# The first row of experts in another order: units 2 and 3 ahead of the two that are summed by tokens

## The chip, the cores and the metric

One Trainium2 chip, one of its NeuronCores. The metric is the device time of one execution in microseconds, as the median of several runs.

## What is computed

The reference is a small language-model tower over 8 rows (batches) of 512 tokens: an embedding with a decaying memory and four residual MLP layers of width 128; an output head to 64 features; linear attention with four heads; and a mixture of 8 experts, of which each token takes the best two. The change touches the experts alone:

```python
logits = jnp.einsum('bsd,de->bse', xn, Wr) + br
top_vals, top_idx = jax.lax.top_k(logits, K)
w = jax.nn.softmax(top_vals, axis=-1)
w_full = jnp.einsum('bsk,bske->bse', w, jax.nn.one_hot(top_idx, E, dtype=w.dtype))
y = jnp.zeros(x.shape[:-1] + (DOUT,), x.dtype)
for e in range(E):
    h = jax.nn.gelu(jnp.einsum('bsd,dh->bsh', xn, W1[e]) + b1[e], approximate=False)
    y_e = jnp.einsum('bsh,hd->bsd', h, W2[e]) + b2[e]
    y = y + y_e * w_full[..., e, None]
```

Every expert is computed for every token and weighted by its gate, which is zero for the six that were not chosen.

## The kernel before

The program is written out by hand, one instruction stream for each engine: TensorE (PE), VectorE (DVE), ScalarE (ACT), GpSimd (POOL) and SyncE, which issues the DMAs. The streams wait for each other by semaphores, and each engine works strictly in the order in which its stream is written. From the span's start to about 265 us the tower runs, then the attention of the eight rows, and from about 304 us the experts.

A **unit** is one expert of one row of 512 tokens: unit `n` is row `n // 8`, expert `n % 8`, 64 in all. An ordinary unit takes these steps:

- `hidden(n)` on PE: two 128x512 products with the high and the low part of the first weights, into bank 4 or 0 by turns. It waits until the gelu of unit n-2 has emptied its bank.
- `gelu(n)` on ACT (line 898), out of that bank.
- `spread_gates(n)` on PE: the expert's gates, spread over all 128 partitions by one 128x512 product with a selection column, into bank 2 or 3 by turns in the first two rows. It waits until the multiplication of the unit before it in that bank is done.
- `dve_job(n)` on DVE (line 1419): hidden times gates.
- `hidden_hi(n)` on ACT (line 904): the product rounded to fp32r.
- `hidden_lo(n)`: the remainder of the rounding, on DVE (line 1426) for even experts and on POOL (line 650) for odd ones.
- `second_products(n)` on PE: two 128x512 products, of the high and of the low part, added up over the experts of a row in bank 6 or 7. The row's `bias_sum` has to come first, since it opens that sum.

The streams go through laps, one for each unit. In lap `n` PE spreads the gates of unit n, issues `hidden(n + 6)` and the second products of unit n - 4 (SKEW is 4, LEAD is 6), and ACT does `gelu(n + 6)` and then the rounding of unit n - 1.

Four units are exceptions (`ALONE`): 0 and 1 at the start of the first row, and the last two of the last row. For these there is no spread, no multiplication, no rounding. PE multiplies the unrounded hidden values by the second weights with the tokens on the partitions (`alone_product`, here ahead of lap 0), into the two halves of bank 6, and DVE adds each with its gate per token straight to the output row (`alone_sum`, line 1445, four instructions). `alone_taken` says that DVE has done so. Since bank 6 is also the one in which row 0 adds up its experts, `bias_sum(0)` must wait for both sums.

In the kernel before, laps 0 and 1 have no spread and no multiplication, laps 4 and 5 have the two `alone_sum` on DVE and no second products on PE, and `bias_sum(0)` stands in lap 6. Around these laps the last work of attention is interleaved: `projected_context(7)`, `q_transposes(7)`, `attend(6)` and `attend(7)` on PE, `scaled_output(5)`, `residual_moments(5)` and `scaled_m(7)` on DVE (lines 1315, 1167 to 1170, 1301), the norm of row 5 on POOL, and the transposes of the gates of row 1 (`turn_gates(1)`, in lap 4).

Of the kernel before, what the change touches and what calls it, by code (L numbers as in the profile page):

```python
# [34 lines left out]
B, S, V = 8, 512, 64  # L35
# [9 lines left out]
SKEW = 4  # L45
# [32 lines left out]
UNITS = B * E  # L78
# [59 lines left out]
def alone(n):  # L138

    return n in ALONE  # L140


def alone_before(n):
# [49 lines left out]
def build(nc, tok_in, emb_in, wupd_in, wf_in, w1_in, w2_in, headw_in, cols_in, rows_in, cons_in,  # L193
          wqkv_in, wout_in, memv_in, wr_in, ew1_in, ew2_in, eb2_in, out_hbm):
    ctx = ExitStack()
    with ctx:
# [472 lines left out]
        def _(act):  # L669
# [277 lines left out]
            for n in range(UNITS + SKEW + 2):  # L947
                m, u = divmod(n, E)
                if u == SKEW + 1 and n >= E:
                    copy_sum(m - 1)  # L950
                if n + LEAD < UNITS:
                    gelu(n + LEAD)
                if 1 <= n <= UNITS and split(n - 1):
                    hidden_hi(n - 1)
                if n == 2:
                    q_turned(7, 1)
                if n == 5:
                    output_squares(6, 0)
                if n in (7, 8):
                    ez_of(5, 1, pair(n - 7))  # L960
                if n == E + 1:
                    ez_hi(5, 1)
                    output_squares(7, 1)
                if n == E + 5:
                    expert_z_turned(5)
                if n in (2 * E - 1, 2 * E):
                    ez_of(6, 0, pair(n - (2 * E - 1)))
                if n == 2 * E + 1:
                    ez_hi(6, 0)
                if n in (2 * E + 6, 2 * E + 7):  # L970
                    ez_of(7, 1, pair(n - (2 * E + 6)))
                if n == 2 * E + 7:
                    expert_z_turned(6)
                if n == 3 * E:
                    ez_hi(7, 1)
                if n == 4 * E - 3:
                    expert_z_turned(7)
                if n == 2 * E + 4:
                    gate(1)
                if n == 5 * E:  # L980
                    gate(2)
                if n in GATES_AT:
                    copy_gates(GATES_AT.index(n) + 1)
# [3 lines left out]
        def _(dve):  # L987
# [512 lines left out]

            for n in range(UNITS + E + 1):
                m, u = divmod(n, E)
                if n < UNITS and not alone(n):
                    dve_job(n)
                if n in (4, 5):
                    alone_sum(n - 4)
                if n == 1:
                    scaled_output(5, 1)
                if n == 2:
                    residual_moments(5, 1)  # L1510
                    scaled_m(7, 1, v_total[7])
                if n == 6:
                    output_sums(6, 0)
                if n == E:
                    scaled_output(6, 0)
                if n == E + 1:
                    residual_moments(6, 0)
                if n == E + 2:
                    expert_z_lo(5, 1)
                    output_sums(7, 1)  # L1520
                if n == E + 5:
                    scaled_output(7, 1)
                if n == E + 6:
                    residual_moments(7, 1)
                if n == 2 * E + 2:
                    expert_z_lo(6, 0)
                if n == 3 * E + 1:
                    expert_z_lo(7, 1)
                if n in (2 * E + 1, 4 * E + 3):
                    p = 1 if n < 3 * E else 2  # L1530
                    take_logits(p)
                    v = first_max(p)
                if n in (2 * E + 2, 4 * E + 5):
                    v = first_hot(p, v)
                if n in (2 * E + 3, 4 * E + 6):
                    v = second_max(p, v)
                if n in (2 * E + 4, 4 * E + 7):
                    v = second_hot(p, v)
                if n in (2 * E + 5, 5 * E + 1):
                    v = weights(p, v)  # L1540
                if n in (2 * E + 6, 5 * E + 2):
                    gates_out(p, v)
                if u == 0 and n == UNITS + E:
                    alone_sum(UNITS - 2)
                    alone_sum(UNITS - 1)
                if u == 0 and n >= 2 * E:
                    output(m - 2)
                if 1 <= n <= UNITS and lo_by_dve(n - 1):
                    hidden_lo(n - 1)


        @block.tensor
        def _(pe):
# [454 lines left out]
            for n in range(UNITS + SKEW + 4):  # L2008
                m, u = divmod(n, E)
                if n < UNITS:  # L2010
                    if u == 0:
                        pe.wait_ge(gates_copied, m + 1)
                    if n == E + SKEW:
                        pe.wait_ge(h1_ready, 7)
                    if not alone(n):
                        spread_gates(n)
                if n + LEAD < UNITS:
                    hidden(n + LEAD)
                if n == SKEW + 2:
                    pe.wait_ge(alone_taken, 2)  # L2020
                if n == SKEW + 2 or (u == SKEW and 0 < m < B):
                    bias_sum(m * E)
                if n == 0:
                    projected_context(7, 1)
# [5 lines left out]
                    attend(7, 1)  # L2030
                if n in GATES_AT:
                    turn_gates(GATES_AT.index(n) + 1)
                if SKEW <= n < UNITS + SKEW and not alone(n - SKEW):
                    second_products(n - SKEW)
                if n in (UNITS - 3, UNITS - 2):
                    alone_product(n + 1)
                if u == SKEW + 3 and n >= E:
# [75 lines left out]
```

## Time and profile before

| | us |
|---|---|
| median of 3 runs | 414.32 |
| lowest and highest of them | 412.72, 414.88 |
| the profiled execution's own time | 413.41 |
| its span in the trace | 411.6 |
| PE, DVE, ACT, POOL busy in it | 387.6, 351.5, 322.0, 257.1 |

The span runs from the first to the last instruction that the profile holds; 1.8 us lie around it. A row of a timeline gives the start in us from the span's start, how long the row's instructions took from the first start to the last end, the engine, the line, the operation with its output and inputs, their number, and in brackets the idle time ahead of it on that engine with what ended it. Instructions overlap a little, so the distance between two starts is shorter than the time of one. A row of a table of stretches gives the stretch, its length, then for PE, the loading of PE's weights, DVE, ACT and POOL the busy us with the number of instructions, then the mean granted clock of PE as a share of full speed, the share of DMA time and GB/s.

### The profile page before, as it was taken

What the parts mean: (1) busy time and instruction counts of PE and PEld (TensorE: products, weight loads), DVE (VectorE), ACT (ScalarE), POOL (GpSimd) and SP (SyncE); (2) the same over time, 40 slices, a digit from 0 to 9 for tenths busy, and PEclk for the clock granted to TensorE, in tenths of its full rate; (3) what the DMA queues carried; (4) which work ended last, traced back from release to release, by engine and by line L of the source; (5) the groups of instructions that cost most, each with busy time, mean ns of one, the idle gap of its engine ahead of it and who ended that gap; (6) DMA issues with size and microseconds to landing.
All of it is one profiled execution on the core that took longest, in us unless ns stands there. A gap on an engine that the chain in (4) does not pass through costs nothing.

```text
span 411.6 us, 6417 instructions
## 1 busy us (share of the span) xinstructions
PE 387.6 (94%) x2005; PEld 314.3 (76%) x2005; DVE 351.5 (85%) x863; ACT 322.0 (78%) x552; POOL 257.1 (62%) x386
## 2 busy tenths in 40 slices
PE   5698899999999999999999998999998899999995
PEld 2496578888888888888888887877887677786774
DVE  4887798888988898898888979999986899889886
ACT  1263599989999998898887765578787898997983
POOL 0575787778778879877787466586521554545451
PEclk9999999999999999999999999999999999999998
DMA  6900002212121211221222000000000000000001
GB/s 200 362 7 0 2 26 41 38 52 53 36 41 53 52 30 51 51 41 38 53 51 52 2 0 2 1 2 1 2 0 2 1 2 13 15 13 13 15 13 26
DMA packets 15850, 14.94 MB, mean 36 GB/s; under 512 B 9797, under 2 KB 10569, under 8 KB 15561
## 3 DMA queue, kind: packets, MB, share of 16 engines
q1 hardware_dynamic: 15816, 14.54, 14.0%
q8 instruction: 16, 0.26, 0.3%
q14 instruction: 18, 0.14, 0.1%
HBM read 13.42 MB, written 1.11 MB: 35 GB/s over the span
## 4 chain that ended last, share of the span: by engine, by line
PE 65%; DVE 18%; ACT 7%; issue 5%; DMA 3%; SPq 2%; POOL 0%; DVEq 0%; ACTq 0%
PE ps L1555 59%; PE ps L1578 4%; DMA hh<-in_tokens 3%; DVE hid L1419 2%; ACT w_all L904 2%; DVE x L1419 1%; ACT x L898 1%; DVE stats L1034 1%; DVE kstat L1255 1%; ACT hid L898 1%; SPq L451 1%; DVE x L1271 1%; DVE hh L1445 1%; DVE hh L1315 1%; DVE qmax L1267 1%
## 5 line engine op out<-in xcount | busy, mean ns | idle before, releaser
L1108 DVE TENSOR_TENSOR hid_lo<-hid,hid_hi 128x1024 fp32r<-128x1024 f32 x64 | 79.1, 1235 | 25.5 <-ACT hid_hi L742 25.4
L737 ACT ACTIVATE hid<-ps,b_fold 128x512 f32<-128x512 f32 x128 | 83.8, 681 | 20.3 <-PE ps L1555 19.9
L1555 PE MATMUL ps<-xn_hi,w_all 128*128 128x512 f32 x256 | 87.7, 403 | 0.7 <-DVE xn_lo L1103 0.6
L1555 PE MATMUL ps<-hid_hi,w_all 128*128 128x512 f32 x256 | 85.0, 393 | 0.0
L742 ACT ACTIVATE hid_hi<-hid 128x1024 fp32r<-128x1024 f32 x64 | 67.9, 1061 | 2.0
L1555 PEld LDWEIGHTS ps<-xn_hi,w_all 128*128 128x128 f32 x256 | 48.4, 189 | 11.2 <-issue 0.9
L1555 PEld LDWEIGHTS ps<-hid_hi,w_all 128*128 128x128 f32 x256 | 48.1, 188 | 9.9
L1555 PE MATMUL ps<-xn_lo,w_all 128*128 128x512 f32 x128 | 50.0, 390 | 0.0
L1555 PE MATMUL ps<-hid_lo,w_all 128*128 128x512 f32 x128 | 49.8, 389 | 0.0
L1555 PE MATMUL ps<-hid_hi,ew 128*128 128x512 f32 x128 | 40.6, 400 | 1.0 <-ACT memT L840 0.4
L1034 DVE BATCH_NORM_STATS2 stats<-ps 128x6 f32<-128x128 f32 x160 | 35.1, 280 | 3.3 <-PE ps L1578 3.3
L542 POOL TENSOR_TENSOR var_in<-var_in 128x4 f32<-128x4 f32 x30 | 34.2, 1141 | 2.4
L546 POOL TENSOR_TENSOR var_in<-var_in,mhalf 128x4 f32<-128x4 f32 x30 | 31.4, 1047 | 2.3
L538 POOL TENSOR_TENSOR var_in<-stats 128x4 f32<-128x4 f32 x30 | 17.2, 573 | 24.4 <-DVE stats L1034 24.4
L1578 PEld LDWEIGHTS ps<-cons,x 128*128 128x128 f32 x160 | 23.2, 187 | 9.8 <-DVE x L1053 4.4
L1578 PE MATMUL ps<-cons,x 128*128 128x128 f32 x160 | 25.4, 281 | 4.4 <-DVE x L1053 3.2
L1555 PE MATMUL ps<-w_all,ew 128*128 128x512 f32 x77 | 28.7, 413 | 0.8 <-DVE xn_lo L1426 0.2
L1555 PEld LDWEIGHTS ps<-hid_hi,ew 128*128 128x128 f32 x128 | 23.5, 188 | 6.8 <-ACT x L898 0.8
L1555 PEld LDWEIGHTS ps<-hid_lo,w_all 128*128 128x128 f32 x128 | 24.0, 188 | 4.8
L1555 PEld LDWEIGHTS ps<-xn_lo,w_all 128*128 128x128 f32 x128 | 24.1, 189 | 4.0
L904 ACT ACTIVATE w_all<-hid 128x512 fp32r<-128x512 f32 x39 | 24.8, 638 | 2.1 <-DVE hid L1419 2.0
L1555 PE MATMUL ps<-hid_lo,sel 128*128 128x512 f32 x60 | 25.4, 423 | 0.8 <-ACT hid_lo L884 0.4
(237 smaller groups left out, 914.5 us busy)
## 6 DMA issues: line engine op xcount, KB each, us to landing
rstd_row<-roots SPq DMA_DIRECT2D x29, 256.0 KB, 3.8
hh<-in_tokens SPq DMA_DIRECT2D x8, 256.0 KB, 8.3
hid<-in_w SPq DMA_DIRECT2D x1, 1024.0 KB, 7.7
rstd_row<-in_w SPq DMA_DIRECT2D x1, 1024.0 KB, 10.6
out<-hh SPq DMA_DIRECT2D x7, 128.0 KB, 2.0
ew_raw<-in_expert_w SPq DMA_DIRECT2D x1, 512.0 KB, 9.7
roots<-rstd SPq DMA_DIRECT2D x29, 2.0 KB, 1.4
ew_raw<-in_expert_w SPq DMA_DIRECT2D x1, 256.0 KB, 9.9
```

The costliest lines, as they stand in the source:

```text
L538: own.inc(pool.tensor_tensor(vi[:, 0, :], st[:, :, 1], st[:, :, 4], ALU.subtract))
L542: own.inc(pool.tensor_tensor(vi[:, 0, :], vi[:, 0, :], vi[:, 0, :], ALU.mult))
L546: v = own.inc(pool.tensor_tensor(vi[:, 0, :], vi[:, 2, :], mhalf[:, 0:NT], ALU.pow))
L737: act.activation(hid[:, j % 2, f, :], bank[f], ACT.Gelu, bias=b1_fold[:, j // B * F + f:j // B * F + f + 1]).then_inc(gelu_done, 1)
L742: act.activation(hid_hi[:, j % 2, 2 * p:2 * p + 2, :], hid[:, j % 2, 2 * p:2 * p + 2, :], ACT.Copy).then_inc(hhi_ready, 1)
L898: act.activation(hg(n % NHG), bank[HIDDEN_BANK[n % 2]], ACT.Gelu, bias=eb1_fold[:, n % E:n % E + 1]).then_inc(eg_done, 1)
L904: act.activation(hw_hi[:, slot * S:(slot + 1) * S], hw(slot), ACT.Copy).then_inc(hwhi_act, 1)
L1034: last = dve.bn_stats(stats6[:, slot, t, :], bank[TB][:, t * P:(t + 1) * P])
L1108: dve.tensor_tensor(hid_lo[:, j % 2, 2 * p:2 * p + 2, :], hid[:, j % 2, 2 * p:2 * p + 2, :], hid_hi[:, j % 2, 2 * p:2 * p + 2, :].bitcast( ...
L1419: dve.tensor_tensor(hw(slot), hg(n % NHG), bank[spread_bank(n)], ALU.mult).then_inc(hw_ready, 1)
L1555: return pe.matmul(out, lhsT, rhs, start=start, stop=stop)
L1578: last = pe.transpose(bank[TB][:, t * P:(t + 1) * P], part, ident)
```

## The change

A new function, `unit_at(n)`, says which unit lap n takes: 2, 3, 0, 1 for laps 0 to 3, and n from there on. The spread, the multiplication, the rounding, the remainder (on DVE; on POOL it skips units 0 and 1 anyway) and the second products go by it. So laps 0 and 1 have the spread and the multiplication of units 2 and 3, laps 2 and 3 have the two sums by tokens, and laps 4 and 5 of PE have the second products of 2 and 3. `bias_sum(0)`, with its wait for both sums, moves from lap 6 to lap 4. `hidden` and `gelu` keep their order.

```diff
+def unit_at(n):
+
+    return (2, 3, 0, 1)[n] if n < 4 else n
...
-                if 1 <= n <= UNITS and split(n - 1):
-                    hidden_hi(n - 1)
+                if 1 <= n <= UNITS and split(unit_at(n - 1)):
+                    hidden_hi(unit_at(n - 1))
...
-                if n < UNITS and not alone(n):
-                    dve_job(n)
-                if n in (4, 5):
-                    alone_sum(n - 4)
+                if n < UNITS and not alone(unit_at(n)):
+                    dve_job(unit_at(n))
+                if n in (2, 3):
+                    alone_sum(unit_at(n))
...
-                if 1 <= n <= UNITS and lo_by_dve(n - 1):
-                    hidden_lo(n - 1)
+                if 1 <= n <= UNITS and lo_by_dve(unit_at(n - 1)):
+                    hidden_lo(unit_at(n - 1))
...
-                    if not alone(n):
-                        spread_gates(n)
+                    if not alone(unit_at(n)):
+                        spread_gates(unit_at(n))
                 if n + LEAD < UNITS:
                     hidden(n + LEAD)
-                if n == SKEW + 2:
+                if n == SKEW:
                     pe.wait_ge(alone_taken, 2)
-                if n == SKEW + 2 or (u == SKEW and 0 < m < B):
+                if u == SKEW and m < B:
                     bias_sum(m * E)
...
-                if SKEW <= n < UNITS + SKEW and not alone(n - SKEW):
-                    second_products(n - SKEW)
+                if SKEW <= n < UNITS + SKEW and not alone(unit_at(n - SKEW)):
+                    second_products(unit_at(n - SKEW))
```

What this does to the order of PE's stream between `hidden(9)` and the first second products. `hid_hi,ew1` is a `hidden`, `hid_lo,sel` a spread, `hid_lo,eb2` the bias sum, `cons,w_all` the transposes of gates, `mx_sb,qT` the attention product, `w_all,ew2` and `xn_lo,ew2` the second products. All lines are 5 higher in the changed kernel. Before:

```order
L1555 MATMUL ps<-hid_hi,ew1 128x512 x2
L1555 MATMUL ps<-hid_lo,sel 128x512
L1555 MATMUL ps<-hid_hi,ew1 128x512 x2
L1880 MATMUL ps<-cons,w_all 128x128 x4
L1555 MATMUL ps<-hid_lo,sel 128x512
L1555 MATMUL ps<-hid_hi,ew1 128x512 x2
L1555 MATMUL ps<-mx_sb,qT 128x2x64 x4
L1555 MATMUL ps<-hid_lo,sel 128x512
L1555 MATMUL ps<-hid_hi,ew1 128x512 x2
L1555 MATMUL ps<-hid_lo,eb2 128x512
L1555 MATMUL ps<-w_all,ew2 128x512
L1555 MATMUL ps<-xn_lo,ew2 128x512
```

In the changed kernel, from the same `hidden(9)` on:

```order
L1560 MATMUL ps<-hid_hi,ew1 128x512 x2
L1560 MATMUL ps<-hid_lo,sel 128x512
L1560 MATMUL ps<-hid_hi,ew1 128x512 x2
L1560 MATMUL ps<-hid_lo,eb2 128x512
L1885 MATMUL ps<-cons,w_all 128x128 x4
L1560 MATMUL ps<-w_all,ew2 128x512
L1560 MATMUL ps<-xn_lo,ew2 128x512
L1560 MATMUL ps<-hid_lo,sel 128x512
L1560 MATMUL ps<-hid_hi,ew1 128x512 x2
L1560 MATMUL ps<-mx_sb,qT 128x2x64 x4
L1560 MATMUL ps<-w_all,ew2 128x512
L1560 MATMUL ps<-xn_lo,ew2 128x512
```

The bias sum, ninth piece behind `hidden(9)` before, is now the third; the transposes, two spreads, `hidden(11)`, `hidden(12)` and the attention product, which stood ahead of it, stand behind it.

DVE's stream from the scaled output of row 5 (line 1315) to the remainder of unit 4. Line 1419 is a multiplication, 1426 a remainder, 1445 a sum by tokens, 1167 and 1170 the moments. Before:

```order
L1315 SCALAR_TENSOR_TENSOR hh<-ps,r2,hh 128x64 x4
L1419 TENSOR_TENSOR hid<-hid,ps 128x512
L1167 BN_STATS st1<-hh 128x6 x4
L1170 BN_AGGR mv1<-st1 128x2 x4
L1301 SCALAR_TENSOR_TENSOR mx_sb<-ps,kstat,bout_share 128x128
L1419 TENSOR_TENSOR hid<-hid,ps 128x512
L1426 TENSOR_TENSOR xn_lo<-hid,w_all 128x512
L1419 TENSOR_TENSOR x<-x,ps 128x512
L1445 SCALAR_TENSOR_TENSOR hh<-ps,gate_half,hh 128x64 x4
L1419 TENSOR_TENSOR x<-x,ps 128x512
L1445 SCALAR_TENSOR_TENSOR hh<-ps,gate_half,hh 128x64 x4
L1426 TENSOR_TENSOR w_all<-x,w_all 128x512
```

In the changed kernel:

```order
L1424 TENSOR_TENSOR hid<-hid,ps 128x512 x2
L1320 SCALAR_TENSOR_TENSOR hh<-ps,r2,hh 128x64 x4
L1431 TENSOR_TENSOR xn_lo<-hid,w_all 128x512
L1450 SCALAR_TENSOR_TENSOR hh<-ps,gate_half,hh 128x64 x4
L1172 BN_STATS st1<-hh 128x6 x4
L1175 BN_AGGR mv1<-st1 128x2 x4
L1306 SCALAR_TENSOR_TENSOR mx_sb<-ps,kstat,bout_share 128x128
L1450 SCALAR_TENSOR_TENSOR hh<-ps,gate_half,hh 128x64 x4
L1424 TENSOR_TENSOR x<-x,ps 128x512 x2
L1431 TENSOR_TENSOR w_all<-x,w_all 128x512
```

Both multiplications and the remainder of unit 2 now stand ahead of the first sum by tokens, and the multiplications of units 4 and 5 behind the second.

## Rows read from the trace of the kernel before

**Rows 1.** The table of stretches, three of the expert stage.

```profile
323.00:331.00 8.00, 7.84 (x40) 6.17 (x39) 6.87 (x22) 6.59 (x15) 4.15 (x4) 1.00 0.00 1
331.00:343.00 12.00, 11.93 (x58) 9.62 (x59) 11.50 (x33) 11.86 (x24) 8.95 (x14) 1.00 0.05 12
...
379.00:391.00 12.00, 11.23 (x50) 8.18 (x50) 10.65 (x20) 10.80 (x20) 6.30 (x5) 1.00 0.07 16
```

**Rows 2.** PE's timeline, laps 0 to 2 (hidden 4 to the spread of 2).

```profile
312.48 1.16 PE L1555 MATMUL ps<-hid_hi,ew 128*128 128x512 f32 x4
314.06 0.70 PE L1555 MATMUL ps<-hid_hi,ew 128*128 128x512 f32 x2 [0.41 <-ACT x L898]
...
315.03 0.73 PE L1555 MATMUL ps<-hid_hi,ew 128*128 128x512 f32 x2
315.60 0.39 PE L1555 MATMUL ps<-hid_lo,sel 128*128 128x512 f32 x1
315.83 0.63 PE L1555 MATMUL ps<-hid_hi,ew 128*128 128x512 f32 x2
```

**Rows 3.** PE's timeline, laps 4 to 12.

```profile
318.13 0.60 PE L1880 MATMUL ps<-cons,w_all 128*128 128x128 f32 x4
318.60 0.49 PE L1555 MATMUL ps<-hid_lo,sel 128*128 128x512 f32 x1
...
319.39 1.05 PE L1555 MATMUL ps<-mx_sb,qT 128*128 128x128 f32 x8
320.21 0.50 PE L1555 MATMUL ps<-hid_lo,sel 128*128 128x512 f32 x1
...
322.71 0.50 PE L1555 MATMUL ps<-hid_lo,eb 128*128 128x512 f32 x1 [1.53 <-DVEq L1449]
323.05 0.40 PE L1555 MATMUL ps<-w_all,ew 128*128 128x512 f32 x1
...
331.07 0.47 PE L1555 MATMUL ps<-hid_lo,sel 128*128 128x512 f32 x1 [0.23 <-DVE x L1419]
```

**Rows 4.** DVE's timeline, laps 0 to 10.

```profile
312.42 0.85 DVE L1315 SCALAR_TENSOR_TENSOR hh<-ps,r,hh 128x64 f32<-128x64 f32 x4
316.10 0.69 DVE L1419 TENSOR_TENSOR hid<-hid,ps 128x512 f32<-128x512 f32 x1 [2.83 <-PE ps L1555]
316.70 0.60 DVE L1167 BATCH_NORM_STATS2 st<-hh 128x6 f32<-128x64 f32 x4
...
317.63 0.32 DVE L1301 SCALAR_TENSOR_TENSOR mx_sb<-ps,kstat,bout_share 128x128 f32<-128x128 f32 x1
...
321.75 0.85 DVE L1445 SCALAR_TENSOR_TENSOR hh<-ps,gate_half,hh 128x64 f32<-128x64 f32 x4
...
330.24 0.68 DVE L1419 TENSOR_TENSOR x<-hid,ps 128x512 f32<-128x512 f32 x1
```

**Rows 5.** ACT's timeline, laps 1 to 8.

```profile
315.80 0.69 ACT L898 ACTIVATE x<-ps,eb_fold 128x512 f32<-128x512 f32 x1 [0.24 <-PE ps L1555]
...
322.22 0.66 ACT L904 ACTIVATE w_all<-x 128x512 fp32r<-128x512 f32 x1
324.41 0.69 ACT L898 ACTIVATE x<-ps,eb_fold 128x512 f32<-128x512 f32 x1 [1.52 <-PE ps L1555]
324.99 0.62 ACT L904 ACTIVATE w_all<-hid 128x512 fp32r<-128x512 f32 x1
325.51 0.76 ACT L862 ACTIVATE ezf<-hh,s_shift,s 128x64 f32<-128x64 f32 x2
```

**Rows 6.** POOL's timeline, the remainder of unit 3.

```profile
320.01 1.29 POOL L650 TENSOR_TENSOR xn_lo<-hid,w_all 128x512 fp32r<-128x512 f32 x1 [0.39 <-ACT w_all L904]
```

**Rows 7.** The table of stretches, one early and two at the end.

```profile
19.00:21.00 2.00, 0.52 (x5) 0.52 (x6) 2.00 (x6) 0.00 (x0) 1.27 (x6) 1.00 0.47 173
408.00:409.50 1.50, 0.00 (x0) 0.00 (x0) 1.28 (x6) 0.00 (x0) 0.00 (x0) 1.00 0.01 1
409.50:410.00 0.50, 0.00 (x0) 0.00 (x0) 0.05 (x1) 0.00 (x0) 0.00 (x0) 0.51 0.05 12
```

## Prediction

> **What bounds the kernel now.** I read the busy time by stretches first, then the timeline of each engine around the head of the expert stage, then the waits in brackets there. TensorE (PE) is busy 11.93 of 12.00 us from 331 on, and still 11.23 in its emptiest later stretch before the end, from 379 [rows 1]: the time at which it gets to 331 is carried to the end, unless its few later waits shrink. ScalarE (ACT) is nearly as full, 11.86 of 12.00 between 331 and 343 [rows 1]. The slack lies ahead of that, at the laps that the change rewrites. There VectorE (DVE) idles 2.83 us until the spread of unit 2 is there [rows 4], PE idles 1.53 us until DVE has taken the two sums by tokens and bank 6 is free [rows 3], and ACT idles 1.52 us behind that stall of PE until gelu 13 has its product [rows 5]. These three gaps are what can be won or lost. All the work is kept: 2005 matmuls before, as many after, and no DMA is touched.
>
> I number work by unit: "multiply 2" is DVE's multiplication of unit 2 by its spread gates, "rounding 2" ACT's copy of it to fp32r, "remainder 2" the subtraction on DVE or GpSimd (POOL), "hidden 8" PE's two first products.
>
> **The head: spreads and multiplies of 2 and 3.** The spread of unit 2 now stands behind hidden 4 and 5. That row starts at 312.48 and its four matmuls take 1.16 us [rows 2], so the last one starts at about 313.3 and the spread, one slot of 0.23 us later (315.60 to 315.83), at 313.5. It fills a hole: hidden 6 started at 314.06 after 0.41 us idle, since it waits for gelu 4 [rows 2], and will start there still. From a spread's start to its multiply are 0.50 us (315.60 on PE, 316.10 on DVE) [rows 2, 4]. Multiply 2 so starts at 314.0 rather than 316.10. The spread of unit 3 stands where hidden 7 stood, at 315.0 [rows 2], and multiply 3 starts at 315.5. Hidden 7 goes back 0.2 us and hidden 8 goes forward, as no spread stands between them now. PE loses nothing here.
>
> **DVE up to the second sum by tokens.** After multiply 3 (0.60 us to the next, from 316.10 to 316.70 [rows 4]) DVE is at 316.1. The scaled output of row 5, which stood ahead at 312.42 and took 0.85 us [rows 4], comes next: 316.9. Remainder 2 is now ahead of the sums, and waits for rounding 2, which ACT has directly behind gelu 7: 315.80 plus 0.58 (gelu to next start, 324.41 to 324.99) plus 0.66 of its own [rows 5], so 317.1. Remainder 2 ends at 317.7. The first sum by tokens takes 0.86: 318.56. The moments of row 5 take 0.93 (316.70 to 317.63): 319.5. One more operation, 0.32 long [rows 4], brings 319.75. The second sum holds DVE for 0.85 us, and PE's bias product started 0.96 us after it began (321.75 and 322.71) [rows 3, 4], so bank 6 is free at **320.7**, 2.0 us sooner than before. That is what the change gains.
>
> **What stands behind that wait on PE.** PE's wait for bank 6 moves from lap 6 to lap 4. Before, PE had issued everything through hidden 12 when it stopped. Now it stops right behind hidden 10, which ended its issue at 318.13 [rows 3]: a stall of 2.6 us rather than 1.53. Behind it are queued the transposes of gates (0.47, 318.13 to 318.60), the spread of unit 5 and hidden 11 (0.79, to 319.39), the attention product of row 6 (0.82, to 320.21), and the spread of 6 with hidden 12 (0.97, from there to the start of the idle time at 321.18) [rows 3]. That is 3.05 us of which about 0.15 is the last matmul's own end. PE frees the bank wait 2.0 us sooner and owes 2.9 us more behind it. On PE alone that is a loss of 0.8 to 0.9 us.
>
> **What that does to ACT, and so to DVE.** Both are fed by what PE now holds back. After 320.7 come the bias product 0.34 (322.71 to 323.05), the gates 0.47, the products of unit 2 0.47 and the spread of 5 0.23, so hidden 11 starts at 322.2. Attention follows at 322.7 and ends its issue at 323.5. Products of unit 3 and the spread of 6 (0.47 and 0.33) put hidden 12 at 324.3. A gelu starts 0.77 us after its first product (315.03 and 315.80) [rows 2, 5]: gelu 12 at 325.1. Rounding 5 and gelu 13 follow at 0.58 and 0.52 (324.41, 324.99, 325.51 [rows 5]): gelu 13 at **326.1**, where it was at 324.41 [rows 5]. ACT is 1.7 us late, and it has no idle time to give: the 1.41 us that it idled between 323 and 331 is this one gap, and after it the share is 11.86 of 12.00 [rows 1, 5]. So roundings 6 and 8, remainders 6 and 8 behind them on DVE, and multiply 10 (330.24, now 331.9) come 1.7 us late. PE's spread of unit 12 waits for multiply 10 to free its bank: it started at 331.07 after 0.23 us idle [rows 3, 4], and will start near 332.8. From there PE is full and carries it to the end.
>
> **Sum.** Minus 2.0 for the earlier bank, plus 2.9 for PE's work behind it, plus 0.8 by which ACT's chain of gelu 12, rounding 5 and gelu 13 ends later than PE's own loss: **plus 1.7 us**, 0.4%. The profiled execution took 413.41 us for a span of 411.6, and would take 415.1. It is 0.9 us below the median of the runs, 414.32, which would become 416.0. I name the middle, **415.5 us**.
>
> Costs taken as nothing: POOL's remainder 3 stands behind the norm of row 5, whose moments come 1.7 us later. It would start at 321.8 rather than 320.01 and take 1.29 [rows 6], ending at 323.1; products 3 reach PE at about 323.5. That cover is 0.4 us, and if it is gone each 0.1 us is lost on PE. The scaled output moved back by 3.7 us frees a bank that the attention product of row 6 needs only after 322. The drain of DVE's queue behind a sum lies in the 0.96; the first sum's could add 0 to 0.1.
>
> **Rivals.**
> *Absorbed later.* The later waits of PE could take the delay in. The stretch from 379 to 391 has 0.77 us without a matmul [rows 1], and if PE's lateness is shorter there than what DVE and ACT are ahead, the loss is eaten. Against it: those waits are for DVE and ACT too, which are as late as PE. Time: plus 0 to 0.9, so 414.3.
> *Faster.* What binds could be DVE, whose idle time falls from 2.83 to 1.6 us at the head [rows 4]. If remainder 2 finds its rounding in time and multiply 3 its spread, the sums end 1.1 us sooner than reckoned, at 319.6, and PE's stall is 1.5 us, no longer than now. If then gelu 13 catches up by the 0.5 us that ACT's stops between gelu 11 and 12 are worth, ACT is at par, and the earlier multiplies pull 1.2 us out of DVE. Time: 412.9. The point that decides is bank 6 free before 319.3.
> *A second stall.* Multiply 5 now waits for a spread that stands behind the bank wait, remainder 3 for the norm on POOL. If the DVE queue takes these on top of ACT's lateness (multiply 5 at 322.4, since its spread starts at 322.0, and the POOL cover of 0.4 gone), PE's spread of unit 12 slips 0.8 us further: plus 2.5, 416.4.
> *The clock.* PE would stand idle for 2.6 us in one piece. The trace shows it at work for only 0.52 of the 2.00 us from 19 to 21 with the granted clock at 1.00 throughout; at the end no matmul runs from 408.0 on, the clock is still 1.00 until 409.5 and 0.51 of full behind it [rows 7]. So a fall after a stall of this size can't be excluded. If the clock fell from 2.4 to 1.2 GHz behind it, PE's slots would double until it rose: with 2 to 4 us of work in that state 2 to 4 us are lost on top, and the time is 417.5 to 419.5. The Trainium skill ("TensorE: Matmul & The Clock Gate", the table of "Why this matters for your kernels") asks for no long idle gap between bursts of matmuls, else the clock drops to half; by that rule the change stretches the worst gap of this stage, and the trace agrees so far as its end shows the drop, and shows that the 1.5 us around 20 did no harm.
> *The change could fail to do what it says:* no; the order on each engine, shown above, is moved as described.
>
> **Chances.** Forecast (plus 1.0 to 2.3) 0.60, absorbed 0.17, second stall 0.10, clock 0.07, faster 0.06. A measurement of this kernel can tell about 0.5%, 2.1 us, from no change. Slower by more than that: the clock, the second stall for the most part, and a fifth of the forecast, in all 0.28. Faster by more: most of the faster case stays within the bound, and 0.05 is left. The same: 0.67. The range of 413.7 to 417.3 holds the forecast on either base, the absorbed case and the second stall, and leaves out the clock and the faster case.
>
> **What would show it.** Multiply 2 near 314.0 on DVE. PE's longest idle time in this stage 2.2 to 2.9 us, ending with the bias product near 320.7. Gelu 13 near 326.1 and PE's spread of unit 12 near 332.8, and from there the same rows as before, shifted by one constant. It is wrong if the stall is under 1.8 us, if gelu 13 starts before 325.3, if the shift at 343 is gone at 400, or if a slice of the clock between 318 and 330 is under 1.00.

## The result, and the profile after

| | before | changed |
|---|---|---|
| median of 18 runs each, us | 413.26 | 416.80 |
| lowest and highest, us | 412.72, 415.10 | 414.69, 419.23 |
| ratio of the times, with its 95% interval | | 1.0077 [1.0059, 1.0095] |
| the profiled execution: time, span, us | 413.41, 411.6 | 419.23, 417.4 |
| its mean granted clock of PE | 0.997 | 0.989 |

The change makes the kernel slower by 0.8%, 3.5 us between the medians. With 18 runs the median of before is 413.26, a microsecond under the one from three runs that the prediction started from.

The page of the changed kernel: its span, the busy times, and PE with its granted clock in 40 slices of 10.4 us each.

```profile
span 417.4 us, 6416 instructions
## 1 busy us (share of the span) xinstructions
PE 391.2 (94%) x2005; PEld 316.6 (76%) x2005; DVE 352.1 (84%) x863; ACT 322.3 (77%) x552; POOL 257.1 (62%) x386
...
PE   4799899999999999999999999999996999999995
...
PEclk9998999999999999999999999999999899999998
```

The number of matmuls is the same, 2005, and PE is busy 3.6 us longer with them. Two slices of the clock have an 8, the fourth and the one at 323; the kernel before has none in its page but the last. This profiled execution is the slowest of the 18, so it has to be read in two parts.

**Ahead of the rewritten laps it is already 2.57 us late.** Hidden 4 starts at 315.05 (below), where it started at 312.48 [rows 2]. PE's timeline near the start shows the first loss, in code that the change does not touch:

```profile
7.42 0.59 PE L1560 MATMUL ps<-cols,cons 128*128 128x1 f32 x2 [1.98 <-DMA xn<-in_w_f]
```

The same row began at 6.17 before, so a load came 1.3 us later. The second is the clock, in the table of stretches:

```profile
28.00:33.00 5.00, 4.58 (x33) 3.96 (x32) 3.64 (x12) 2.61 (x4) 2.65 (x5) 0.97 0.00 0
33.00:38.00 5.00, 5.00 (x29) 4.45 (x28) 3.44 (x8) 0.00 (x0) 2.53 (x6) 0.69 0.00 0
```

```profile
32.78 1.09 PE L1583 MATMUL ps<-cons,x 128*128 128x128 f32 x4 [0.42 <-DVE stats L1039]
```

The clock fell here behind an idle time of 0.42 us, in a stretch of which PE worked 4.58 of 5.00 us. The kernel before has the same 0.42 us at 31.80 and no fall behind it. Both losses stand in code that the change does not touch. The profile of experiment 7 has the same early fall; the load is late in none of the others by more than the 0.45 us of experiment 5. So I count everything from hidden 4 on, and take 2.57 off when I compare with the prediction's times.

**In the rewritten laps.** PE's timeline of the changed kernel:

```profile
315.05 1.16 PE L1560 MATMUL ps<-hid_hi,ew 128*128 128x512 f32 x4
316.05 0.40 PE L1560 MATMUL ps<-hid_lo,sel 128*128 128x512 f32 x1
...
320.20 0.73 PE L1560 MATMUL ps<-hid_hi,ew 128*128 128x512 f32 x2
323.35 0.79 PE L1560 MATMUL ps<-hid_lo,eb 128*128 128x512 f32 x1 [2.42 <-DVEq L1454]
323.94 1.06 PE L1885 MATMUL ps<-cons,w_all 128*128 128x128 f32 x4
324.65 0.78 PE L1560 MATMUL ps<-w_all,ew 128*128 128x512 f32 x1
...
326.63 1.05 PE L1560 MATMUL ps<-mx_sb,qT 128*128 128x128 f32 x8
...
336.96 0.47 PE L1560 MATMUL ps<-hid_lo,sel 128*128 128x512 f32 x1 [0.77 <-DVE x L1424]
```

PE stands still for 2.42 us behind hidden 10, where it stood 1.53 us behind hidden 12 [rows 3]. What follows is slow: from the transposes of gates to the next piece are 0.71 us here (323.94 to 324.65), and were 0.47 before (318.13 to 318.60) [rows 3]. The table of stretches says why:

```profile
321.00:322.00 1.00, 0.00 (x0) 0.00 (x0) 0.82 (x7) 1.00 (x3) 0.00 (x0) 1.00 0.00 0
322.00:323.00 1.00, 0.00 (x0) 0.00 (x0) 1.00 (x9) 0.32 (x1) 0.60 (x3) 0.93 0.00 0
323.00:324.00 1.00, 0.65 (x2) 0.53 (x3) 0.79 (x3) 0.00 (x0) 0.92 (x2) 0.50 0.00 0
324.00:325.00 1.00, 1.00 (x6) 1.00 (x5) 0.14 (x1) 0.00 (x0) 1.00 (x2) 0.50 0.00 0
325.00:326.00 1.00, 1.00 (x3) 0.79 (x3) 0.00 (x0) 0.60 (x1) 0.32 (x1) 0.50 0.00 0
326.00:327.00 1.00, 1.00 (x7) 0.84 (x6) 0.62 (x1) 0.17 (x1) 0.00 (x0) 0.86 0.00 0
...
331.00:343.00 12.00, 11.02 (x53) 8.24 (x52) 11.01 (x37) 11.79 (x25) 8.71 (x12) 1.00 0.01 2
379.00:391.00 12.00, 11.35 (x49) 7.66 (x47) 11.24 (x28) 9.25 (x18) 5.31 (x4) 1.00 0.05 13
```

The third number from the right is the granted clock. It is full while PE idles, falls from 2.4 to 1.2 GHz just before the bank comes free, and PE then works through the pieces that were queued behind its wait at half the clock, until a little after 326. From 327 on the clock is at 1.00 again. From 331 PE is busy 11.02 of 12.00 us, less than the 11.93 of before [rows 1]; 0.77 us of this is the wait of unit 12's spread, the last row of PE's timeline. From 379 it is 11.35, against 11.23.

DVE and ACT in the same laps. First DVE, then ACT:

```profile
316.55 0.69 DVE L1424 TENSOR_TENSOR hid<-hid,ps 128x512 f32<-128x512 f32 x1 [1.46 <-ACT x L903]
318.17 0.69 DVE L1424 TENSOR_TENSOR hid<-hid,ps 128x512 f32<-128x512 f32 x1 [0.93 <-ACT x L903]
...
319.61 0.69 DVE L1431 TENSOR_TENSOR xn_lo<-hid,w_all 128x512 fp32r<-128x512 f32 x1
...
322.39 0.85 DVE L1450 SCALAR_TENSOR_TENSOR hh<-ps,gate_half,hh 128x64 f32<-128x64 f32 x4
323.45 0.69 DVE L1424 TENSOR_TENSOR x<-x,ps 128x512 f32<-128x512 f32 x1 [0.21 <-DVE hh L1450]
326.38 0.69 DVE L1424 TENSOR_TENSOR x<-x,ps 128x512 f32<-128x512 f32 x1 [2.25 <-PE ps L1560]
```

```profile
325.03 0.60 ACT L889 ACTIVATE hid_lo<-ps 128x512 fp32r<-128x512 f32 x1 [2.72 <-PE ps L1885]
326.83 0.69 ACT L903 ACTIVATE hid<-ps,eb_fold 128x512 f32<-128x512 f32 x1 [1.20 <-PE ps L1560]
...
328.90 0.69 ACT L903 ACTIVATE x<-ps,eb_fold 128x512 f32<-128x512 f32 x1 [0.58 <-PE ps L1560]
...
330.01 0.68 ACT L903 ACTIVATE x<-ps,eb_fold 128x512 f32<-128x512 f32 x1
```

DVE has broken its one idle time of 2.83 us [rows 4] into 1.46 and 0.93, and then waits 2.25 us for the spread of unit 5, which stands behind PE's wait. ACT waits three times for PE (2.72, 1.20, 0.58) where it waited 1.52 once [rows 5]; gelu 13 is the last row. POOL's remainder of unit 3 started here:

```profile
324.05 1.27 POOL L655 TENSOR_TENSOR xn_lo<-hid,w_all 128x512 fp32r<-128x512 f32 x1
```

Counted from hidden 4, gelu 13 comes 3.0 us later than before (14.96 against 11.93), the spread of unit 12 3.3 us later (21.91 against 18.59), and the end of the span 3.25 us later (102.35 against 99.1). What is lost up to the spread of unit 12 is neither won back nor added to.

### The profile page after: what moved, and what is told of

It reads as the page before. It is cut to its first block, busy times and chain, and to the rows that moved or that the text cites. A ratio compares the mean times of both kernels' runs of the same rounds, so it can differ in the third digit from the quotient of the medians.

```text
span 417.4 us, 6416 instructions
## 1 busy us (share of the span) xinstructions
PE 391.2 (94%) x2005; PEld 316.6 (76%) x2005; DVE 352.1 (84%) x863; ACT 322.3 (77%) x552; POOL 257.1 (62%) x386
## 4 chain that ended last, share of the span: by engine, by line
PE 66%; DVE 18%; ACT 8%; issue 5%; DMA 1%; POOL 1%; SPq 1%; DVEq 0%; ACTq 0%
PE ps L1560 59%; PE ps L1583 4%; ACT w_all L909 2%; ACT x L903 1%; DVE hid L1424 1%; DVE stats L1039 1%; DVE hh L1320 1%; DMA xn<-in_w_f 1%; DVE kstat L1260 1%; ACT hid L903 1%; DVE x L1276 1%; DVE hh L1450 1%; PE ps L1591 1%; DVE x L1424 1%; DVE qmax L1272 1%
```

## The experiments

**The theories.** *Order*: the wait for bank 6, with the second products of units 2 and 3 behind it, stands two laps too early in PE's stream, and the work queued behind it costs 1.7 us, as forecast. *Clock*: the idle time in one piece lets the granted clock fall, and that is the rest. *DVE*: what costs is the new order on DVE, where a multiplication now waits behind the sums. Against these: the loss is not in these laps at all. The times of before are 413.26 (413.35 for experiments 7 and 8), each ratio with its 95% interval. "Counted" means from the start of hidden 4 in the profiled run, in which before has 10.23 for the bias sum, 11.93 for gelu 13, 18.59 for the spread of unit 12 and 99.1 for the end.

**1. PE kept busy ahead of the wait.** The changed kernel with eight extra products into bank 7, whose result nobody reads, in the idle time.

```diff
                 if n == SKEW:
+                    pe.wait_ge(h1_ready, 6)
+                    for _ in range(8):
+                        mm(bank[7], ew1[:, 0, 0:P], row_of(z_all, 0))
                     pe.wait_ge(alone_taken, 2)
```

> The changed kernel with eight matmuls of 512 columns more on TensorE, into a bank that is free, right ahead of its wait for the two sums by tokens. They fill about 1.9 of the 2.42 us that it idles there. Theory (order and clock): the order costs 1.6 us whatever the clock does, and the rest, on average 1.9 us of the measured 3.5, is the granted clock at 0.50 behind the stall. Then the clock stays at 1.00 in the expert stage, the time is 1.6 us above the kernel before (ratio 1.004, 414.9 us) and the runs lie closer together. Rival (the order alone costs all): the ratio stays near 1.0077. Second rival (eight matmuls more only push everything back): above 1.0077.

Measured: 415.23 us, ratio 1.0055 [1.0040, 1.0070], five of six runs at 415.1 to 416.1 with a mean clock of 0.997 or more. PE's timeline:

```profile
317.48 2.59 PE L1560 MATMUL ps<-hid_hi,ew 128*128 128x512 f32 x10
320.63 0.50 PE L1560 MATMUL ps<-hid_lo,eb 128*128 128x512 f32 x1 [0.56 <-DVEq L1454]
320.96 0.61 PE L1885 MATMUL ps<-cons,w_all 128*128 128x128 f32 x4
...
322.12 0.63 PE L1560 MATMUL ps<-hid_hi,ew 128*128 128x512 f32 x2
322.58 1.05 PE L1560 MATMUL ps<-mx_sb,qT 128*128 128x128 f32 x8
```

Idle time 0.56, no slice of the clock below 1.00 here. Behind the wait this is the changed kernel without the clock, and its rows can be held against the forecast. Counted, the bias sum is at 8.31, hidden 11 at 9.80, gelu 13 at 13.63 (1.70 later than before), the spread of unit 12 at 20.59 (2.00 later), the end at 101.1 (2.0 later). The Order part stands by itself at about 2 us. The same stretch gives the price of the clock: from the bias sum to the attention product are 1.95 us here and 3.28 in the changed kernel's profile (323.35 to 326.63), 1.33 more for the same pieces.

**2. Only three extra products.** Experiment 1 with `range(3)`, so that some 1.7 us stay idle.

```diff
-                    for _ in range(8):
+                    for _ in range(3):
```

> The changed kernel with three instead of eight matmuls more ahead of the wait: TensorE idles 1.7 to 1.8 us rather than 2.42 or 0.56. The order costs 1.6 us as ever, so the ratio is 1.004 if the clock holds in all runs and 1.0077 if it falls as often as in the changed kernel. Theory: it holds in most, as it does in the kernel before behind 1.53 us of idle time, ratio 1.004 to 1.005. Rival (any stall over about 1.6 us is enough): 1.007.

Measured: 415.96 us, ratio 1.0041 [1.0009, 1.0072]. The twelve runs fall into two groups with nothing between: six at 415.02 to 415.37, all with a mean clock of 0.998 or more, six at 416.55 to 416.94, all at 0.993 to 0.995. The profiled run is of the second, first its PE timeline, then its stretches:

```profile
317.65 1.43 PE L1560 MATMUL ps<-hid_hi,ew 128*128 128x512 f32 x5
320.79 0.79 PE L1560 MATMUL ps<-hid_lo,eb 128*128 128x512 f32 x1 [1.71 <-DVEq L1454]
...
324.30 1.05 PE L1560 MATMUL ps<-mx_sb,qT 128*128 128x128 f32 x8
```

```profile
319.00:321.00 2.00, 0.29 (x2) 0.21 (x1) 1.75 (x13) 0.76 (x2) 1.16 (x3) 0.95 0.00 0
321.00:322.00 1.00, 1.00 (x4) 0.87 (x5) 0.58 (x1) 0.00 (x0) 0.92 (x3) 0.50 0.00 0
```

The clock fell behind 1.71 us of idle time, and the pieces from the bias sum to the attention product took 3.51 us, 1.56 more than in experiment 1. The two groups lie 1.6 us apart. So 1.7 us can be enough, and it is not certain to be. The clock held in half of the runs, not in most as expected.

**3. Bias sum and second products back where they were.** The changed kernel with PE's wait, the bias sum and the second products as before; the new order stays for spreads, multiplications, roundings and the sums by tokens.

```diff
-                if n == SKEW:
+                if n == SKEW + 2:
                     pe.wait_ge(alone_taken, 2)
-                if u == SKEW and m < B:
+                if n == SKEW + 2 or (u == SKEW and 0 < m < B):
                     bias_sum(m * E)
...
-                if SKEW <= n < UNITS + SKEW and not alone(unit_at(n - SKEW)):
-                    second_products(unit_at(n - SKEW))
+                if SKEW <= n < UNITS + SKEW and not alone(n - SKEW):
+                    second_products(n - SKEW)
```

> The changed kernel with the bias sum, its wait, and the second products of units 2 and 3 back in laps 6 and 7, as before; spreads, multiplications and sums by tokens stay in the new order. Theory (the wait stands too early on TensorE): bank 6 is free near 320.7 on the old time axis and TensorE reaches its wait near 321.2, so the stall of 1.53 us is gone and the kernel is 0.7 us faster than before (ratio 0.998), since ScalarE has two roundings more ahead of gelu 8 and 9 and gives part of it back. Rival (the new order of spreads and multiplications is itself the cost): it stays slower than before by 1 us or more.

Measured: 412.95 us, ratio 0.9991 [0.9981, 1.0001], no mean clock under 0.997 in twelve runs. Counted, the bias sum is at 9.96 without any idle time ahead of it, the spread of unit 12 at 18.43, the end at 99.0. The whole loss is gone once PE's early wait and its early second products are back; the new order on DVE costs nothing, and the DVE theory falls. This run does not say how much belongs to the wait and how much to the products. It also wins next to nothing, 0.3 us where 0.7 were expected, since PE now waits 0.60 us for multiply 4 instead (the spread of unit 6 needs its bank), and 0.42 us ahead of the transposes.

**4. The sums by tokens first, in the kernel before.** DVE's two sums go into its idle time ahead of multiply 2.

```diff
-                dve.wait_ge(alone_done, k + 1)
+                dve.wait_ge(alone_done, max(k + 1, 2))
...
+                if n == 0:
+                    alone_sum(0)
+                    alone_sum(1)
                 if n < UNITS and not alone(n):
                     dve_job(n)
-                if n in (4, 5):
-                    alone_sum(n - 4)
```

> The kernel before with one thing changed: VectorE does both sums by tokens in lap 0, ahead of the first multiplication, where it idles 2.83 us. Theory: the 1.7 us of work goes into idle time, bank 6 is free near 315, TensorE's wait of 1.53 us in lap 6 is gone, and 1.4 us reach the end, as ScalarE and TensorE are full behind it: ratio 0.9966, 411.9 us. Rival (the time is bound elsewhere, the stall was cover for ScalarE): no difference.

Measured: 412.49 us, ratio 0.9976 [0.9960, 0.9992]. Faster by 0.24%, and in the profile by 1.35 us counted to the end (97.75). The seven runs with a mean clock of 0.997 or more have their median at the expected 411.9; the other five, at 0.994 or 0.995, lie at 412.99 to 413.71. In this kernel PE has no idle time over 0.54 us in these laps, so where their clock fell is open. DVE's timeline:

```profile
312.18 0.85 DVE L1445 SCALAR_TENSOR_TENSOR hh<-ps,gate_half,hh 128x64 f32<-128x64 f32 x4
313.25 0.86 DVE L1445 SCALAR_TENSOR_TENSOR hh<-ps,gate_half,hh 128x64 f32<-128x64 f32 x4 [0.21 <-DVE hh L1445]
314.32 0.86 DVE L1315 SCALAR_TENSOR_TENSOR hh<-ps,r,hh 128x64 f32<-128x64 f32 x4 [0.21 <-DVE hh L1445]
315.87 0.69 DVE L1419 TENSOR_TENSOR hid<-hid,ps 128x512 f32<-128x512 f32 x1 [0.69 <-PE ps L1556]
```

The idle time of 2.83 us [rows 4] is down to 0.69 with both sums in it, multiply 2 is where it was, and PE's bias sum finds its bank free. The three gaps that the prediction named can be closed, by moving the sums rather than the units.

**5. The same in the changed kernel,** with PE's stream as changed (the edit of experiment 4 on `n in (2, 3)`).

> The changed kernel with the sums by tokens in lap 0 of VectorE ahead of the multiplications. TensorE's wait in lap 4 is then over before it is reached. Theory (the wait in lap 4 is the whole cost): no stall over 1 us, the clock stays at 1.00, and the kernel stands within 0.3 us of the kernel before (ratio 1.000), as the products of unit 3 now wait 0.9 us for GpSimd. Rival (what costs is the new order on ScalarE and VectorE, not the wait): 1 us or more above the kernel before.

Measured: 413.54 us, ratio 1.0003 [0.9982, 1.0024]. With the bank free in time (bias sum counted at 5.74, without any idle time ahead of it) PE's early wait costs nothing, as Order says. But the gain of experiment 4 is gone too: the spread of unit 12 is at 18.87, 0.28 later than before, and the end at 99.4. The first kernel of experiment 6 differs from this one only in that the bias sum and the second products of 2 and 3 stand two laps later on PE; its spread of unit 12 is at 17.57 and its end at 98.1. So with the bank free the early products cost 1.3 us. Hidden 11 and 12 stand behind them, and ACT waits 0.38 and 1.18 us for these two here, and no more than 0.18 us there; PE also waits 0.33 us for POOL's remainder 3. Part of the changed kernel's loss must be of this kind.

**6. Experiments 3 and 4 together,** and the same with roundings and remainders of 2 and 3 in their old places.

```diff
-                if 1 <= n <= UNITS and split(unit_at(n - 1)):
-                    hidden_hi(unit_at(n - 1))
+                if 1 <= n <= UNITS and split(n - 1):
+                    hidden_hi(n - 1)
...
-                if 1 <= n <= UNITS and lo_by_dve(unit_at(n - 1)):
-                    hidden_lo(unit_at(n - 1))
+                if 1 <= n <= UNITS and lo_by_dve(n - 1):
+                    hidden_lo(n - 1)
```

> The new order of spreads, multiplications and roundings, with the products of 2 and 3 and the bias sum back in laps 6 and 7 and both sums by tokens in lap 0 of VectorE. Theory (only the place of the sums against TensorE's wait counts): as good as the sums alone in lap 0, ratio 0.9975 (412.3 us), because with the stall gone the new order itself is worth nothing. Rival (the earlier multiplications are worth something once nothing waits for bank 6): ratio under 0.9965.

> As the one with both, but ScalarE's roundings and VectorE's remainders of units 2 and 3 stay in laps 3 and 4, as before; only the spreads and multiplications of 2 and 3 and the sums by tokens are early. Theory (the roundings ahead of gelu 8 and 9 hold back hidden 10): 0.3 to 0.4 us faster than with both, ratio 0.9965 (411.8 us), the best of the set. Rival: no difference to the sums alone in lap 0.

Measured: 412.35 us, ratio 0.9961 [0.9935, 0.9986], and 411.84 us, ratio 0.9959 [0.9929, 0.9990]. Both beat both kernels, but their intervals hold experiment 4's ratio too, so these runs cannot say that the new order of units adds anything to the sums in the idle time. Leaving the roundings where they were is worth 0.5 us between these two (0.3 to 0.4 expected), and 0.57 in the profiles, counted to the end (97.53 against 98.1); their intervals overlap as well. In the second one's DVE timeline both sums stand as in experiment 4, the first at 312.43, and multiplications 2 and 3 start right behind them at 314.57.

**7. The wait one lap later.** The changed kernel with the wait and the bias sum in lap 5 rather than 4, and the products of units 2 and 3 in laps 5 and 6: half of the way back to experiment 3.

```diff
-                if n == SKEW:
+                if n == SKEW + 1:
                     pe.wait_ge(alone_taken, 2)
-                if u == SKEW and m < B:
+                if n == SKEW + 1 or (u == SKEW and 0 < m < B):
                     bias_sum(m * E)
...
+                if n in (SKEW + 1, SKEW + 2):
+                    second_products(n - SKEW + 1)
+                if SKEW + 4 <= n < UNITS + SKEW and not alone(n - SKEW):
+                    second_products(n - SKEW)
```

> The changed kernel with the bias sum, its wait, and the products of units 2 and 3 one lap later on TensorE (laps 5 and 6, so behind the transposes of gates, the spread of 5, hidden 11 and the attention product where the order of the lap has them so). Theory (each piece queued behind the wait in lap 4 costs its own length): the stall falls from 2.42 to 0.8 to 1.1 us, the clock holds, and the kernel stands within 0.3 us of the kernel before, ratio 1.000. Rival (the early multiplications are the cost): still 1.6 us slower, 1.004.

Measured: 413.72 us, ratio 1.0008 [0.9993, 1.0024]. Nine of twelve runs are at 413.34 to 413.81, against 413.3 for before's runs without a fall. PE's timeline:

```profile
320.60 0.63 PE L1885 MATMUL ps<-cons,w_all 128*128 128x128 f32 x4 [0.42 <-issue]
...
321.30 0.63 PE L1560 MATMUL ps<-hid_hi,ew 128*128 128x512 f32 x2
322.59 0.49 PE L1560 MATMUL ps<-hid_lo,eb 128*128 128x512 f32 x1 [0.65 <-DVEq L1454]
```

With the transposes, a spread and hidden 11 ahead of the wait, 0.65 us of the stall is left, and counted to the end the loss is 0.4 us (99.5). One lap makes most of the difference: 2.0 us with three pieces more behind the wait, 0.4 without them. The second products of unit 2 moved by that lap too.

**8. The changed kernel again,** as it is, on the same chip as experiment 7, since its profiled run had been its slowest.

> The changed kernel again, to set beside the others on the same chip. By the theory its runs fall in two groups: those with a mean granted clock of 0.997 or more near 414.9 us, and those with one or two falls of the clock near 416.6 and 417.8, more of the second than the kernel before has. Rival (the earlier runs were this high by chance of that chip): the median is near 414.9.

Measured: 415.42 us, ratio 1.0053 [1.0033, 1.0072]. Four of six runs at 415.13 to 415.59 with mean clocks of 0.997 and 0.998, two at 416.55 and 416.90 with 0.993 and 0.994. The profiled one is the 416.55. It has no early loss (hidden 4 at 312.29), and behind the stall:

```profile
320.59 0.80 PE L1560 MATMUL ps<-hid_lo,eb 128*128 128x512 f32 x1 [2.41 <-DVEq L1454]
...
323.94 1.05 PE L1560 MATMUL ps<-mx_sb,qT 128*128 128x128 f32 x8
```

```profile
319.00:321.00 2.00, 0.41 (x1) 0.41 (x2) 1.75 (x11) 0.56 (x1) 1.35 (x3) 0.80 0.00 0
321.00:322.00 1.00, 1.00 (x6) 0.87 (x5) 0.38 (x1) 0.00 (x0) 0.92 (x3) 0.50 0.00 0
```

The same stall, the same fall: 3.35 us from the bias sum to the attention product, 1.40 more than in experiment 1. The two groups of runs are 1.5 us apart.

**9. A longer stall in the kernel before.** Two additions on DVE on a table that nobody reads afterwards, ahead of the second sum, so that the bank comes free 1.5 us later.

```diff
+                if n == 5:
+                    for _ in range(2):
+                        own.wait(own.inc(dve.tensor_tensor(
+                            ew1_g[:, 0:S], ew1_g[:, 0:S], ew1_g[:, S:2 * S], ALU.add)))
                 if n in (4, 5):
                     alone_sum(n - 4)
```

> The kernel before with two needless additions of 512 columns on VectorE ahead of the second sum by tokens: some 1.4 us more, so TensorE's stall in lap 6 grows from 1.53 to 2.5 to 2.9 us with the order of the units unchanged. Theory (a stall of that length lets TensorE's clock fall): besides the 1.2 to 1.4 us of the work itself the granted clock is 0.50 for 3.4 us behind the stall in a good part of the runs, and the runs spread from 414.5 to 416.5 us, median ratio 1.006 to 1.008. Rival (the fall in the changed kernel comes from its order or from chance, not from the length of the stall): the clock stays at 1.00 there, ratio 1.003 and the runs lie together.

Measured: 415.66 us, ratio 1.0043 [1.0016, 1.0071]. PE's timeline and stretches of the profiled run, which took 414.81 us:

```profile
324.06 0.50 PE L1558 MATMUL ps<-hid_lo,eb 128*128 128x512 f32 x1 [3.08 <-DVEq L1449]
```

```profile
323.00:324.00 1.00, 0.00 (x0) 0.00 (x0) 0.86 (x4) 0.00 (x0) 1.00 (x1) 1.00 0.00 0
324.00:325.00 1.00, 0.94 (x4) 0.81 (x5) 0.90 (x2) 0.00 (x0) 0.08 (x1) 1.00 0.00 0
```

In this run PE idled 3.08 us and the clock stayed at 1.00. The cost is the length of the stall, no more: 1.55 us on the bias sum (counted 11.78), 1.6 to the end. Four of the twelve runs are like it (414.68 to 414.82, clock 0.998). Six are at 415.65 to 415.94 with 0.995 or 0.996, two at 416.92 and 417.65 with 0.990. So a stall without the early wait costs its own length, and the clock is again lower in most runs, at some 0.9 us; that it falls behind this stall is not shown, since the one profile has no fall. The median ratio lies between the 1.003 of the rival and the 1.006 that the theory asked for.

The runs by their mean granted clock, for the share that had a fall somewhere ahead of the end. The idle time is PE's longest in the profile from hidden 4 to the spread of unit 12.

| kernel | PE's idle time, us | runs with a clock of 0.996 or less | time of the others, us |
|---|---|---|---|
| before (the runs beside all experiments) | 1.53 | 17 of 81 | 412.80 to 414.41 |
| changed | 2.42 | 13 of 18 | 414.69 to 416.29 |
| changed again (8) | 2.41 | 2 of 6 | 415.13 to 415.59 |
| three extra products (2) | 1.71 | 6 of 12 | 415.02 to 415.37 |
| longer stall (9) | 3.08 | 8 of 12 | 414.68 to 414.82 |
| eight extra products (1) | 0.76 | 1 of 6 | 415.08 to 416.07 |
| one lap later (7) | 0.76 | 3 of 12 | 413.34 to 413.81 |
| products as before (3) | 0.60 | 0 of 12 | 412.74 to 414.13 |
| sums first (4) | 0.54 | 5 of 12 | 411.44 to 413.12 |
| changed, sums first (5) | 0.78 | 3 of 12 | 413.08 to 413.78 |
| both (6) | 0.48 | 0 of 12 | 411.56 to 413.33 |
| both, roundings as before (6) | 0.55 | 1 of 12 | 411.32 to 412.50 |

With an idle time of 1.71 us or more 29 of 48 runs have a lower clock, with none over 0.78 us 13 of 78, and in the kernel before 17 of 81. So the long stall makes a fall more likely, and falls come without one too.

## Why the prediction was right, and where it was wrong

Right is the mechanism of the sum, and nearly its size: what PE holds back behind the early wait was put at plus 1.7 us, and is plus 2.0 where the clock does not disturb. Step by step, with 2.57 us taken off the changed kernel's profile, or counted from hidden 4 in experiment 1, where the clock does not disturb.

| step | predicted | measured |
|---|---|---|
| multiply 2, multiply 3 | 314.0, 315.5 | 313.98, 315.60 |
| remainder 2 | 317.1 | 317.04 |
| bank 6 free (bias sum) | 320.7 | 320.78 |
| PE's stall | 2.6 us | 2.42, 2.41 |
| hidden 11, 12 (counted) | 9.7, 11.8 | 9.80, 11.86 |
| gelu 13 against before | +1.7 us | +1.70 in experiment 1, +3.0 with the fall |
| spread of unit 12 | +1.7 us | +2.0 in experiment 1, +3.3 with the fall |
| carried to the end | +1.7 us | +2.0, and +3.25 |

- **The head, DVE, the bank.** Right to 0.1 us. The gain of 2.0 us on bank 6 was there and worth nothing, because the wait had moved by more than that.
- **What stands behind the wait.** Right, and shown for the wait and the second products together: experiment 3 puts both back and the loss is gone, experiment 7 puts them halfway back and 0.4 us are left. The sum had the products' 0.47 us each ahead of hidden 11 and 12; how the loss divides between them and the wait was not measured in the changed kernel. In runs whose clock did not fall the changed kernel lies 1.6 us (414.69, 414.88, 414.89) to 2.0 us (415.1 to 415.3 in experiment 8) above before's 413.2. The spread of unit 12 was mis-sized by 0.3: it waits 0.77 us for its bank, where I carried over the 0.23 of before.
- **Costs taken as nothing.** POOL's remainder 3 ran at 321.48 (predicted 321.8) and its cover held.
- **The step that failed: the clock,** a rival that the sum left out. By its own last sign, a slice of the clock between 318 and 330 under 1.00, the prediction was wrong here. "PE would stand idle for 2.6 us in one piece ... a fall after a stall of this size can't be excluded", with a chance of 0.07, and no term for it in the sum. It fell in both profiles of the changed kernel, and by the clocks of the runs somewhere in 13 of 18 and in 2 of 6, against 17 of 81 before. The evidence was weighed wrongly: I read the early stretch at 0.52 of 2.00 us [rows 7], in which PE idles 1.84 us in one piece, as a sign that an idle time of this size does no harm. It was one draw. The fall comes in some executions of the same instructions and not in others, so one profile without it bounds nothing. The price was set at 2 to 4 us, for which no row was given, and is 1.3 to 1.6 us of PE's time in the three profiles with a fall in these laps. A term of its price by its frequency, 1.5 by a half, would have made the sum some plus 2.4.
- **The rule on idle gaps.** The Trainium skill ("TensorE: Matmul & The Clock Gate", the table of "Why this matters for your kernels") warns of the kind of loss that came: the fall came behind 2.42, 2.41 and 1.71 us. But these are all shorter than the gap from which its table warns, so read strictly it did not speak against the forecast stall of 2.6 us. Here the measurement decides: the clock fell in part of the runs behind shorter gaps, and in experiment 9's profiled run it did not fall behind 3.08 us.
- **The verdict.** By the bound of 0.5% the kernel is slower, which I gave 0.28, and not the same, which I gave 0.67. The forecast of plus 1.7 us is 0.4%, and the clock's 1.5 us took it over the bound. The median of 416.80 lies 1.3 us above the 415.5 named and within the range. That is partly luck: the starting time was 1.1 us too high, and the range was meant to leave the clock's case out. Against before's 413.26 the difference is 3.5 us where 1.7 were forecast, and 2.1 us in the repeat.
- **The rivals.** *Absorbed later* is wrong, no part of the loss was won back. *Faster* is wrong, the bank came free at 320.78 and not before 319.3; DVE's idle time at the head fell to 2.39 us in two pieces, not to the 1.6 that this rival counted. *A second stall*: multiply 5 did wait 2.25 us for its spread, but in experiment 1, without the clock, the spread of unit 12 is only 0.3 us beyond the forecast, not 0.8.

What stays open: how often the fall comes at this stall. A run's mean clock tells that there was a fall, only a profile tells where, and before has early ones too. The changed kernel's 18 runs and the repeat's 6 differ (13 against 2 with a lower clock, medians 416.80 and 415.42), and two runs of the first lie at 416.2 and 416.3 with a clock of 0.997, so with no fall to explain them; a late load as in the first profile would fit and was not seen in them.

## What to carry to other kernels

In a stream that is worked off in order, a wait costs whatever is queued behind it and ready: making its condition true 2 us sooner is no gain if the wait itself moves past more work than that. Work that nobody waits for costs the same way when it moves ahead of work that another engine needs (1.3 us in experiment 5, with the bank free). Put the wait directly ahead of its first consumer, and look for the idle time of the engine that fulfils it: both sums by tokens fitted into DVE's 2.83 us and gave 0.24%, and 0.4% in the kernels that have the new order of units as well. And price an unbroken idle time of PE near 2 us with more than its length: here the clock was lower in 29 of 48 runs with a stall of 1.71 us or more and in 30 of 159 with a shorter one, and a fall cost about 1.5 us in the three profiles that have one behind the stall.

## What the runs showed of the hardware

- The granted clock fell from 1.00 to 0.50 behind 1.71, 2.41 and 2.42 us in which PE did nothing, while the same kernel ran other executions without a fall, as their mean clocks of 0.997 and more show; behind 3.08 us it stayed at 1.00 in one profiled run. Each of these three falls cost 1.3 to 1.6 us. In the profiles of the changed kernel and of experiment 7 it also fell near 32 us, where PE's idle time was 0.42 us. The length of the idle time alone does not decide.
- Eight products that compute nothing, put into the idle time (experiment 1), filled 1.86 of its 2.42 us (0.56 were left). The clock stayed up in the profiled run, and they delayed nothing: the bias sum came at 8.31 counted, against 8.30 in the repeat of the changed kernel without them.
- Behind a sum by tokens (0.85 us long), after which the kernel has DVE wait for its own last instruction, DVE's next instruction starts 0.99 to 1.07 us after the sum's start: 320.07 to 321.14 and 321.75 to 322.74 in the kernel before, 320.22 to 321.21 in the changed one, 312.18 to 313.25 in experiment 4. In the longer cases the profile shows 0.21 us of idle time.
